# Tokenizer kernel: set-up and stage joined in one program per engine, first pixel tile loaded in two halves

## The reference

```python
x = features.reshape(b, c, h, s, w, s)
reduce_feats = x.mean((3, 5)).reshape(b, c, hw).transpose(0, 2, 1)
unf = x.transpose(0, 1, 2, 4, 3, 5).reshape(b, c, hw, n).transpose(0, 2, 3, 1)
q = _ln(reduce_feats, ln_q_w, ln_q_b) @ Wq.T
kv = _ln(unf, ln_kv_w, ln_kv_b) @ Wkv.T
attn = jax.nn.softmax(jnp.einsum('bhpd,bhpnd->bhpn', q * scale, k), axis=-1)
aggre = jnp.einsum('bhpn,bhpnd->bhpd', attn, v)
return reduce_feats + aggre @ proj_w.T + proj_b
```

## Time and profile before

| | |
|---|---|
| median of 3 runs | 729.01 us (727.99 to 730.46) |
| the profiled execution's own time | 729.95 us |
| its span, first to last instruction | 728.1 us |
| mean granted TensorE clock | 0.959 |
| busy: TensorE, VectorE, GpSimd, ScalarE | 87%, 76%, 64%, 63% of the span |
| the tokenizer's running loop | from about 45 to 320 us |

### The profile page before, as it was taken

The page is one execution under the profiler, slowest core; times in us unless marked ns, Lnnn a source line. Parts: engine busy times, 40 slices in busy tenths (PEclk is TensorE's granted clock), DMA queues, the critical chain, the costliest instruction groups (busy, mean ns, idle before and its releaser), DMA issues.

```text
span 728.1 us, 16646 instructions
## 1 busy us (share of the span) xinstructions
PE 633.0 (87%) x5290; PEld 328.6 (45%) x5290; DVE 555.6 (76%) x1053; ACT 461.6 (63%) x931; POOL 465.7 (64%) x448
## 2 busy tenths in 40 slices
PE   1599999999999999996799889885169999999995
PEld 1122222222222222222456555543068788788884
DVE  1278888898988888898469768788367777777873
ACT  0587777777777777751588768674046656665663
POOL 5846888798888888555604545567705556655656
PEclk9999999999999999997899999999569999999998
DMA  8033333333333221000079720001122222222110
GB/s 322 32 117 117 116 116 117 116 116 118 117 116 117 110 101 40 2 12 1 5 130 158 177 93 34 30 29 45 49 62 54 55 54 55 52 50 54 49 36 2
DMA packets 49070, 57.80 MB, mean 79 GB/s; under 512 B 31970, under 2 KB 44788, under 8 KB 46890
## 3 DMA queue, kind: packets, MB, share of 16 engines
q1 hardware_dynamic: 43882, 50.11, 23.2%
q0 software_dynamic: 5120, 6.84, 2.9%
HBM read 50.03 MB, written 10.28 MB: 83 GB/s over the span
## 4 chain that ended last, share of the span: by engine, by line
PE 37%; issue 4%; DVE 3%; POOL 3%; another core or an unknown queue 1%; ACT 1%; DMA 1%; SPq 0%; DVEq 0%; ACTq 0%; POOLq 0%
PE mixed_bank L1877 12%; PE turned0a L1859 3%; PE turned1a L1859 3%; POOL rows_by_group L1153 2%; PE s_proj L1562 2%; PE back_bank L1884 2%; PE s_logits L1656 2%; PE turned0b L1864 1%; PE turned1b L1864 1%; PE s_delta L1584 1%; PE s_proj L1597 1%; PE s_proj L1572 1%; PE s_proj L1596 1%; PE s_ln L1641 1%
## 5 line engine op out<-in xcount | busy, mean ns | idle before, releaser
L1897 POOL DMA_INDIRECT out<-orow,m_rows x96 | 107.4, 1119 | 91.7 <-ACT orow L1842 67.2
L812 PE MATMUL s_proj<-x_px,w_kv 64*64 64x512 f32 x256 | 133.6, 606 | 0.0
L809 PE MATMUL s_proj<-x_px,w_kv 64*64 64x512 f32 x256 | 133.5, 606 | 0.0
L1791 DVE TENSOR_TENSOR m_xs<-m_rows 128x768 f32<-128x768 f32 x96 | 91.3, 952 | 26.7 <-ACT m_rows L1823 21.3
L496 POOL TENSOR_TENSOR pre<-va 128x1024 f32<-128x1024 f32 x32 | 76.2, 2381 | 40.2 <-DVE va L593 40.2
L1153 POOL DMA_INDIRECT rows_by_group<-r_pay,r_slot_i x64 | 69.7, 1089 | 44.8 <-DVE r_slot_i L1476 27.1
L475 POOL TENSOR_TENSOR half_px<-x_px 128x1024 f32<-128x1024 f32 x32 | 75.8, 2369 | 35.1 <-DMA x_px<-in_x 29.3
L1877 PE MATMUL mixed_bank<-m_xsT,m_w_cur 128*64 128x128 f32 x1344 | 88.9, 276 | 4.7 <-issue 4.5
L579 DVE TENSOR_TENSOR qk<-s_proj,q 128x512 f32<-128x512 f32 x128 | 86.6, 679 | 7.6 <-PE s_proj L812 6.3
L593 DVE TENSOR_TENSOR va<-b_a,v_sb 128x512 f32<-128x512 f32 x128 | 84.9, 685 | 8.0 <-PE b_a L827 7.9
L1877 PEld LDWEIGHTS mixed_bank<-m_xsT,m_w_cur 128*64 128x64 f32 x1344 | 73.9, 137 | 15.1 <-issue 14.8
(11 more groups left out here) (274 smaller groups left out, 1685.7 us busy)
## 6 DMA issues: line engine op xcount, KB each, us to landing
x_px<-in_x SPq DMA_DIRECT2D x16, 2048.0 KB, 8.0
m_rows<-rows_by_group SPq DMA_DIRECT2D x96, 72.0 KB
wt<-in_w2T SPq DMA_DIRECT2D x8, 512.0 KB
rows_by_group<-rows_by_group SPq DMA_DIRECT2D x1, 2286.0 KB
out<-orow,m_rows POOLq DMA_INDIRECT x96
rows_by_group<-r_pay,r_slot_i POOLq DMA_INDIRECT x64
wt<-in_w2T SPq DMA_DIRECT2D x2, 256.0 KB
wt<-in_w2T SPq DMA_DIRECT2D x4, 128.0 KB
```

The source lines that it names most:

```text
L809: mm(b_k[i][LO, :], w_kv[LO, 0, LO], px(t, j, LO), start=True, stop=True)
L812: mm(b_k[i][HI, :], w_kv[HI, 0, HI], px(t, j, HI), start=True, stop=True).then_inc(done["kv_product"], 1)
L1791: d.tensor_tensor(xs[:, i % RING, :, :], rows[:, i, X0:X0 + C].rearrange("p (o c) -> p o c", o=1).broadcast_to([P, UNITS, C]), rows[:, i, ...
L1897: nc.gpsimd.indirect_dma_start(out_d, bass.IndirectOffsetOnAxis(ap=rows[:, i, ID0:ID0 + 1].bitcast(I32), axis=0), orow[:, i, :], None, bou ...
```

## The change

The set-up is no block of its own any more. Its functions are the first ones of the stage's block, so each engine runs from its set-up into its loop without a barrier; the waits that the barrier stood for are written out (`FOLDED` for the weights' folds up to `vec[:, 7:8]`, `SWAPPED` for `e_sw`, `MASKS` for the masks, `x_top` for the first half of tile 0). Tile 0 is loaded by ScalarE in two halves of 32 pixel rows each, before its table load. SyncE loads the vectors and the weights, and issues tiles 1 and 2 only when tile 0 has landed. Tile 0 is pooled by VectorE alone, with one reduction over 16 pixels for each half: the first between `avg_px` and the copies of the products, the second between the folds and the last of them. GpSimd does no `halve` and `quarter` for tile 0; `eps` is set by VectorE. SyncE's refills wait for `pooled` instead of `px_halved`. ScalarE waits for `FOLDED` before its loop.

```diff
--- before
+++ after
@@ set-up, 137 @@
-    LOADS, CENTRED, MASKS = 16 * 6, 8, 32
-    with ExitStack() as wctx:
...
-        with nc.Block(no_gpsimd_drain=True) as block:
-            @block.sync
-            def _(sp):
-                for b in range(2):
-                    sp.dma_start(vec[C * b:C * b + C, 0:5], A["tok_vectors"]).then_inc(loaded, 16)
-                sp.dma_start(x[:, 0, :], x_v[0, :, :]).then_inc(x_in[0], 16)
-                sp.wait_ge(zeroed, 2)
...
-                for t in range(1, NX):
-                    sp.dma_start(x[:, t, :], x_v[t, :, :]).then_inc(x_in[t], 16)
-                sp.wait_ge(loaded, LOADS)
...
-                step(g.memset(eps[:, :], EPS))
...
+    LOADS, CENTRED, MASKS, FOLDED, SWAPPED = 16 * 6, 8, 31, 7, 9
...
+    TOP = PIX // 2
     block = ctx.enter_context(nc.Block(no_gpsimd_drain=True))
+    @block.sync
+    def _(sp):
+        for b in range(2):
+            sp.dma_start(vec[C * b:C * b + C, 0:5], A["tok_vectors"]).then_inc(loaded, 16)
+        sp.wait_ge(zeroed, 3)
...
+            sp.dma_start(w_ld[s, :, s], w).then_inc(loaded, 16)
+            sp.dma_start(w_out[o, s], w[:, 3, :]).then_inc(loaded, 16)
+        sp.wait_ge(x_in[0], 16)
+        for t in range(1, NX):
+            sp.dma_start(x[:, t, :], x_v[t, :, :]).then_inc(x_in[t], 16)
...
+    @block.vector
+    def _(v):
+        nc.vector.memset(w_ld[:, :, :], 0.0).then_inc(zeroed, 1)
+        nc.vector.memset(w_out[:, :], 0.0).then_inc(zeroed, 1)
+        nc.vector.memset(eps[:, :], EPS).then_inc(zeroed, 1)
+
+        def pool_half(h):
+            nc.vector.tensor_reduce(rs2[:, 128 * h:128 * h + 128].rearrange("p (h w) -> p h w", w=TH),
+                                    x[:, 0, TOP * h:TOP * h + TOP].rearrange("p (h s w u) -> p h w s u", s=S, w=TH, u=S),
+                                    AX.XY, ALU.add).then_inc(done["pooled"] if h else top_pooled, 1)
+
+        v.wait_ge(loaded, LOADS)
+        v.wait_ge(masks, CENTRED)
...
+        nc.vector.tensor_scalar(avg_px[:, :], avg[:, :], 1.0 / NP, None, ALU.mult).then_inc(folded, 1)
+        v.wait_ge(x_top, 16)
+        pool_half(0)
+        v.wait_ge(prod, 1)
...
+        nc.vector.tensor_copy(vec[:, 6:7], b_k[1][:, 1:2]).then_inc(folded, 1)
+        v.wait_ge(x_in[0], 16)
+        v.wait_ge(top_pooled, 1)
+        pool_half(1)
+        v.wait_ge(prod, 2)
+        nc.vector.tensor_tensor(vec[:, 7:8], b_v[0][:, 0:1], vec[:, 4:5], ALU.add).then_inc(folded, 1)
+        v.wait_ge(masks, MASKS)
...
@@ slot_free, SyncE's refills @@
-        eng.wait_ge(done["px_halved"], 2 * (tile + 1))
+        eng.wait_ge(done["px_halved"], 2 * tile)
...
-            sp.wait_ge(done["px_halved"], 2 * (t - NX + 1))
+            sp.wait_ge(done["pooled"], t - NX + 1)
@@ ScalarE, start @@
+        act.dma_start(x[:, 0, 0:TOP], x_v[0, :, 0:TOP]).then_inc(x_top, 16)
+        act.dma_start(x[:, 0, TOP:PIX], x_v[0, :, TOP:PIX]).then_inc(x_in[0], 16)
         act.preload_act_table_set("natural_log_exp_and_others")
+        act.wait_ge(x_top, 16)
+        act.wait_ge(zeroed, 3)
+        act.wait_ge(folded, FOLDED)
         for t in range(TILES + 2):
@@ GpSimd halve and quarter, VectorE pool_last @@
-            if not live(t):
+            if not 0 < t < TILES:
                 return
...
@@ VectorE va_mul @@
+            if t == 0 and n == 0:
+                v.wait_ge(folded, SWAPPED)
@@ TensorE kv, spread, mean, q_moments @@
+                if t == 0:
+                    pe.wait_ge(x_top, 16)
...
+            if m == 0:
+                pe.wait_ge(folded, SWAPPED)
...
+            if t == 0:
+                pe.wait_ge(masks, MASKS)
...
+            if t == 0:
+                pe.wait_ge(folded, FOLDED)
```

More of the change, by code:

```diff
@@ L244, in tokenizer @@
     done = {n: sem(n) for n in names.split()}
+    LOADS, CENTRED, MASKS, FOLDED, SWAPPED = 16 * 6, 8, 31, 7, 9
+    zeroed, loaded, masks, scaled, prod, folded, x_top, top_pooled = (sem(n) for n in
+        ("w_zeroed", "w_loaded", "w_masks", "w_scaled", "w_prod", "w_folded", "x_top", "top_pooled"))
+    TOP = PIX // 2
     block = ctx.enter_context(nc.Block(no_gpsimd_drain=True))
+    @block.sync
[3 more added lines that the diff above has]
+        sp.wait_ge(zeroed, 3)
+        for b in range(2):
+            s = slice(C * b, C * b + C)
+            o = slice(C * (1 - b), C * (1 - b) + C)
+            w = A["tok_weights"].rearrange("c (k d) -> c k d", k=4)
+            sp.dma_start(w_ld[s, :, s], w).then_inc(loaded, 16)
[3 more added lines that the diff above has]
+            sp.dma_start(x[:, t, :], x_v[t, :, :]).then_inc(x_in[t], 16)
@@ new lines, in _ @@
+    @block.tensor
+    def _(pe):
+        pe.wait_ge(scaled, 3)
+        pe.wait_ge(masks, CENTRED)
+        for i in range(3):
+            nc.tensor.matmul(b_k[0][:, P * i:P * (i + 1)], cen[:, :], w_sc[:, i, :], start=True, stop=True)
+        nc.tensor.matmul(b_k[1][:, 0:1], w_ld[:, 0, :], vec[:, 1:2], start=True, stop=True)
+        nc.tensor.matmul(b_k[1][:, 1:2], w_ld[:, 2, :], vec[:, 3:4], start=True, stop=True).then_inc(prod, 1)
+        pe.wait_ge(folded, 6)
+        nc.tensor.matmul(b_v[0][:, 0:1], w_ld[:, 3, :], vec[:, 6:7], start=True, stop=True).then_inc(prod, 1)
@@ L472, in halve @@
             s = slice(H2 * h, H2 * h + H2)
-            if t > 0:
-                pool.wait_ge(done["px_quartered"], 2 * (t - 1) + h + 1)
+            if t > 1:
+                pool.wait_ge(done["px_quartered"], 2 * (t - 2) + h + 1)
             g.tensor_tensor(half_px[:, s, :, :], v[:, s, 0:2, :], v[:, s, 2:4, :], ALU.add).then_inc(done["px_halved"], 1)
         def quarter(t, h):
-            if not live(t):
+            if not 0 < t < TILES:
                 return
             s = slice(H2 * h, H2 * h + H2)
-            pool.wait_ge(done["px_halved"], 2 * t + h + 1)
-            if t > 0:
+            pool.wait_ge(done["px_halved"], 2 * t + h - 1)
+            if t > 1:
                 pool.wait_ge(done["pooled"], t)
```

128 lines of the change are left out of this document (48 added, 80 removed).

## The result

The changed kernel takes 720.28 us in the median of 11 runs (715.24 to 724.79), the kernel before in the same sessions 728.07 us (726.18 to 732.78). The ratio is 0.990, with a 95% interval from 0.9873 to 0.9927: faster by 0.7 to 1.3%, some 5 to 9 us. The forecast was 719.7. The profiled execution took 723.42 us around a span of 721.3.

The account below looks back on a forecast made before the run. TensorE paces the loop, so only the start before tile 0's moments can gain: earlier weights and VectorE pooling move these from 26.38 to 17.05, 9.3 us, taking 729.01 to 719.7 us; range 716.0 to 724.2 (8 in 10).

Parts of the forecast that it names:

- What bounds the kernel: Tokenizer: TensorE paces the loop at 18.65 us a tile; only the start before tile 0's moments at 26.38 can gain.
- Loads: Start: tile 0 from ScalarE at 0.80 instead of SyncE at 2.08; weights at 9.0 instead of 11.54, bounds 6.7 to 10.26.
- W: Moment in the start when VectorE has the weights and begins scaling: 11.54 before, forecast 9.0.
- Pooling of tile 0: Start: four GpSimd steps and one VectorE step (17.31 to 25.88) become two VectorE reductions of 2.30 us each.
- rival 2: VectorE's pooling of tile 0: strided reductions run at half rate, 2 x 2.2 us more, 724.1; chance 0.08.
- The order on VectorE from W: Start: scaling and avg_px 0.81 us, then reductions, copies and folds; last fold's product at W + 6.4; moments at 17.05 after ScalarE.
- Edits costed at nothing: Start: table load, eps, the barrier (0.35 us) and its branches cost nothing more, lying in waits that end with W.
- Tile 1: GpSimd's pooling: lands at 17.6, done at 24.9, VectorE wants it at 28.2; slack 3.3 us, hidden.
- 1 (the clock rises sooner): TensorE at the moments and first kv products: shorter idle gap saves 0.96 and as much again, 717.8; chance 0.08.
- 3: Rival, tile 1's load: comes late, in at 23.9, and 3.0 us are lost, 722.7; chance 0.08.
- 4: Rival, later loop: GpSimd's waits for pixel tiles set the pace and the gain is given back, 728.5; chance 0.06.
- 5: Rival, loop: a lower clock doubles one tile's 18.65 us, 738.4; chance 0.04.

Follow-up runs that it names:

- No_gates_warm: no_gates plus 18 products of two constants on TensorE, results unused; 715.64 us, ratio to the kernel before 0.9815.
- tile0_on_sync: Changed kernel, but SyncE issues both halves of tile 0, ahead of the weights; ratio to the kernel before 0.9943, run again 0.9946.
- barrier_back: Changed kernel, but ScalarE, GpSimd and TensorE wait for the whole set-up, as at a barrier; ratio to the kernel before 0.9871.
- square_ungated: Changed kernel without ScalarE's wait for the last fold before its loop; ratio to the kernel before 0.9864.
- one_load: Changed kernel, but tile 0 comes in one load on ScalarE's queue and the first reduction waits for all of it; ratio to the kernel before 0.9936.
- bottom_late: Changed kernel, but ScalarE issues tile 0's second half only when the first has landed; ratio to the kernel before 0.9843.
- all_four: Changed kernel with long mask first, e_sw copied while VectorE idles, ScalarE's square not held back, tile 0's second half late; ratio to the kernel before 0.9834.
- no_gates: Changed kernel, long mask first, ScalarE's square not held back, tile 0's second half and tiles 1, 2 behind SyncE's weights without waits; ratio to before 0.9879.
- changed_again: The changed kernel itself run again as a control; ratio to the kernel before 0.9905.

## Why the prediction was right, and where it was off

- *What bounds the kernel.* Right: the gain arises before 26.38. From the moments to the refill it was 17.2 us before and 17.4 in the changed kernel, so 7.6 of 7.8 us go into the loop, and they arrive: the median fell by 7.8, with an interval of 5 to 9. That what the start gains reaches the end undiminished holds only roughly. No_gates_warm gained 14.75 us up to the refill and 13.4 at the end; tile0_on_sync gained 7.6 and 6.4 in its two profiles and kept 4.5 and 3.2.
- *Loads.* W was 9.73; I took 9.0 and my bounds held. The term was sized by a split between bounds, and the upper, the row of the same loads against the same 2 MB, was the nearer one, as I said and did not follow. Its reason was partly right: a queue of its own brings the weights 1.2 to 1.4 us nearer than tile0_on_sync has them, and 0.7 of that is issue time.
- *Pooling of tile 0.* 2.28 and 2.27 us for my 2.30; rival 2 falls.
- *The order on VectorE from W.* The mechanism was right and one size wrong: "scaling and `avg_px` take 0.81" took until the reduction's start 11.56 - 9.73 = 1.83. I took the row of before, where GpSimd had ended its masks as scaling began, and moved it to a time when it had not. This is 1.0 of the 1.5 us by which the moments came later than my 17.05; W is 0.7, and the rest of the path, 7.0 us for my 7.24, gave 0.2 back. The two are not independent, though: "if only W is off, the sum moves by as much, one for one" is wrong while the long masks run. In the changed kernel twice, barrier_back, square_ungated and one_load W lies between 9.7 and 10.2 and the first reduction starts between 11.56 and 11.75, just behind GpSimd's last long step.
- *Edits costed at nothing.* The barrier is worth 0.9 us by itself with VectorE pooling; the table load, at 1.69, was hidden. The same lock stretched `e_sw`, which I had called harmless; it ended at 20.83, 0.25 us before VectorE's next step, so it was.
- *Tile 1.* Landed at 16.8, its slack was not used up in the changed kernel: VectorE pooled it after waiting for ScalarE, not for GpSimd. In bottom_late, with the moments 3.3 us sooner, VectorE waited 1.6 us for GpSimd instead of 0.96 for ScalarE, without a loss at the refill that could be told; in all_four, 4.4 us sooner, tile 1 binds.
- *Rivals.* 1 (the clock rises sooner) did not come true in the changed kernel: 2.07 us for the moments after a gap of 3.21 us, as before. Its price was about right: from the moments to the refill no_gates_warm takes 2.1 us less than the changed kernel and 2.6 less than no_gates, where I had 1.9. The Trainium skill, page TensorE: Matmul & The Clock Gate, section on the HAM clock gate, agrees in kind: kept busy, the engine works at the upper level. 3 fell; 4 and 5 did not come: the loop keeps 18.65 us a tile and the granted clock reads 1.00 in it.
- *Time.* 719.7 forecast, 720.28 measured; by the terms as measured it would have been 729.01 - 7.6 = 721.4. That the two lie only 0.6 us apart is luck in part: the gain forecast was 9.3 us and the measured one 7.8, and the kernel before ran at 728.07 beside the changed one, 0.9 below the 729.01 that I started from.

## What to carry to other kernels

A duration read in one place holds in another only if what runs beside it is the same: look at the other engines' rows at the new time, GpSimd's beside VectorE's above all. Before a load gets a queue of its own, ask whether it is needed at once: putting off one megabyte brought the weights 2.5 us nearer, and the new queue by itself 1.2, about half of it issue time. And where an engine must idle before the first work on the path, work that it can throw away may be worth more than a shorter set-up.

## What the runs showed of the hardware

- VectorE's scaling of 128x128 tiles and its copies of 128x512 stop for the length of a GpSimd instruction beside them (0.68 to 1.78 us, 0.75 to 3.95 us); its reduction of 128x2048 does not: in bottom_late the first ran from 7.95 for 2.27 us beside a GpSimd step of 1.09 us at 9.16, as long as alone. Where VectorE comes first, GpSimd waits (2.66 us for 2.35 in changed_again).
- A load of 1.2 KB issued together with a load of 1 MB on another queue took 6.1 us to land; issued ahead of tile 0 on the same queue, 2.1 (before) and 1.9 (tile0_on_sync).
- TensorE, given constants to multiply from 3.5 us on and never idle for more than 0.81 us after that, ran the moments in 1.12 us, its upper level; with the set-up's own products alone, the last of them 2.06 us (no_gates) or 3.21 us (changed) before the moments, it took 2.07 us. The profile's clock column reads 1.00 there all the same: the trace has no clock record before the first rise (30.4 us before, 23.0 in the changed kernel), so in the start the level is told by durations.
- One chip ran the kernel before in 698.85 us, others in 728 to 732. On the first no wait was released by an unknown queue, and the scatter took 119.9 us (bottom_late) for 131 to 139; on the others there were 41 to 60 us of such waits over all engines. In tokenizer and start the chips agree: from the first refill to the scatter's start it is 348 to 350 us on all of them.
